# ScalarE's casts behind its copies, and row numbers counted from a partition's first row, in a DLRM tower kernel

## What is computed

```python
e = jnp.stack([tbl_0[ids[:, 0]], ..., tbl_26[ids[:, 26]]], axis=1)   # 2048 x 27 x 128
dot = jnp.einsum('bnd,bmd->bnm', e, e)                              # the pairs i < j are kept: 351
h = jnp.concatenate([pairs, dense_ctx], axis=1)                     # 2048 x 367
h = jnp.maximum(h @ W_top1 + b_top1, 0.0)                           # 512
h = jnp.maximum(h @ W_top2 + b_top2, 0.0)                           # 256
y = h @ W_top3
```

## Time and profile before

| | before |
|---|---|
| median of 3 runs | 383.83 us (383.69 to 386.02) |
| the profiled execution: its time, its span | 381.17 us, 379.3 us |
| PE busy in the span | 345.7 us (91%) |
| PE busy in 0 to 89 us, and in 89 to 363 us | 63.38 us of 89; 271.19 us of 274 |
| VectorE, ScalarE, POOL busy | 294.4, 153.3, 269.3 us |
| ScalarE busy in 0 to 89 us | 37.95 us |
| mean granted clock of PE | 0.987 |

### The profile page before, as it was taken

How to read it: one execution, slowest core, us unless ns; L and a number is a source line. 1 busy time by engine, 2 the same in 40 slices (tenths; PEclk the granted TensorE clock), 3 DMA queues, 4 the chain that set the end, 5 groups by cost and what they waited for, 6 DMA issues and landing times.

```text
span 379.3 us, 9954 instructions
## 1 busy us (share of the span) xinstructions
PE 345.7 (91%) x4035; PEld 322.6 (85%) x4035; DVE 294.4 (78%) x821; ACT 153.3 (40%) x217; POOL 269.3 (71%) x287
## 2 busy tenths in 40 slices
PE   1788868599999999999999999999999999999985
PEld 1677767588999999998999999998999999998874
DVE  4986696898688969798689969798689869793432
ACT  3352644434343453534343453534243453533421
POOL 6777877777777777777777777777777777777400
PEclk9989996999999999999999999999999999999999
DMA  6995225953333333334333333333343343221100
GB/s 184 251 247 136 64 63 137 213 186 96 82 93 85 79 84 82 95 69 95 82 94 85 79 86 81 95 72 91 85 91 85 76 89 83 76 57 50 36 2 1
DMA packets 22988, 36.38 MB, mean 96 GB/s; under 512 B 6224, under 2 KB 17120, under 8 KB 22944
## 3 DMA queue, kind: packets, MB, share of 16 engines
q0 software_dynamic: 8896, 18.24, 20.2%
q1 hardware_dynamic: 14048, 17.52, 18.6%
HBM read 35.73 MB, written 0.01 MB: 94 GB/s over the span
## 4 chain that ended last, share of the span: by engine, by line
PE 75%; POOL 14%; issue 5%; DMA 3%; ACT 2%; DVE 1%; ACTq 0%; DVEq 0%
PE embT_ps L410 35%; PE gram_ps L442 13%; POOL emb L379 12%; PE h_ps L470 11%; PE h_ps L494 7%; PE embT_ps L420 6%; DMA emb<-in_tbl,idx 3%; PE flat_ps L453 2%; POOL flatT L379 2%; ACT embT L634 1%; DVE flat L568 1%; DMA idx<-in_idx_rows 0%; PE h_ps L481 0%; PE flat_ps L481 0%; DVE flat L569 0%
## 5 line engine op out<-in xcount | busy, mean ns | idle before, releaser
L379 POOL DMA_INDIRECT emb<-in_tbl,idx x272 | 261.8, 962 | 83.8 <-issue 80.6
L537 DVE TENSOR_SCALAR one_hot<-ids,row_of 125x256 fp32r<-125x256 int32 x658 | 205.4, 383 | 13.2 <-PE embT_ps L410 10.6
L410 PE MATMUL embT_ps<-one_hot,tbl 125*128 125x256 f32 x1284 | 182.0, 297 | 13.0 <-DVE one_hot L537 11.4
L410 PEld LDWEIGHTS embT_ps<-one_hot,tbl 125*128 125x128 f32 x1284 | 166.7, 196 | 17.9 <-issue 8.9
L634 ACT COPY embT<-embT_ps 128x256 f32<-128x256 f32 x77 | 48.0, 624 | 134.2 <-PE embT_ps L410 129.0
L642 ACT COPY embT<-embT_ps 128x512 f32<-128x512 f32 (+1 forms) x80 | 80.7, 1012 | 11.7 <-PE embT_ps L420 11.7
L568 DVE STREAM_TRANSPOSE flat<-gram_ps 128x864 f32<-128x864 f32 x31 | 33.5, 1082 | 43.7 <-PE gram_ps L442 43.1
L442 PEld LDWEIGHTS gram_ps<-embT 128*59 128x59 f32 x1984 | 56.2, 134 | 9.6 <-ACT embT L634 3.9
L442 PE MATMUL gram_ps<-embT 128*59 128x54 f32 x1984 | 60.2, 217 | 3.8 <-ACT embT L634 2.3
L420 PE MATMUL embT_ps<-ident,emb 128*128 128x128 f32 x272 | 43.8, 276 | 11.6 <-DMA emb<-in_tbl,idx 8.6
L420 PEld LDWEIGHTS embT_ps<-ident,emb 128*128 128x128 f32 x272 | 32.2, 142 | 13.8 <-DMA emb<-in_tbl,idx 11.4
(11 more groups left out here) (47 smaller groups left out, 85.0 us busy)
## 6 DMA issues: line engine op xcount, KB each, us to landing
ids<-in_ids_hot SPq DMA_DIRECT2D x77, 128.0 KB
emb<-in_tbl,idx POOLq DMA_INDIRECT x272, 3.1
embT<-in_tbl SPq DMA_DIRECT2D x5, 448.0 KB
w_sb<-in_tbl SPq DMA_DIRECT2D x3, 560.0 KB
w_sb<-in_W_ring SPq DMA_DIRECT2D x1, 756.0 KB
w_sb<-in_W_top SPq DMA_DIRECT2D x1, 512.0 KB
h1T<-in_tbl SPq DMA_DIRECT2D x1, 448.0 KB
w_sb<-in_tbl SPq DMA_DIRECT2D x1, 448.0 KB
```

The source lines that it names most:

```text
L379: pool.indirect_dma_start(gathered_row(t, s), None, tables[f][:, :], bass.IndirectOffsetOnAxis(ap=idx[:, t, f:f + 1], axis=0),).then_inc(g ...
L410: mm = pe.matmul(out[:, 0:HN], tbl[0:ROWS, part, AT[o] + chunk, :], one_hot[0:ROWS, k % SLOTS, c, :], start=(chunk == 0 and part == 0), st ...
L537: done = dve.tensor_scalar(one_hot[0:ROWS, k % SLOTS, c, :], of, row_of[0:ROWS, KINDS.index(CH[o]), chunk:chunk + 1], None, ALU.is_equal)
```

## The change

Two things are done, both in the first two halves of the samples.

- ScalarE's table casts move. Before, the cast of table n + 3 stood ahead of the copy of hot step n. Now that of table n + 2 stands behind the copy of hot step n; and the casts of tables 5 to 9 stand right behind the copy of hot step 6, 7, 8, 10 and 12, where they stood ahead of the copy of hot step 7, 8, 9, 11 and 13, with the copies of the quads in between.
- For the hot steps 0 to 16, ScalarE rewrites the ids in place: it makes the partition's first row minus the id, as a float (`relative_ids`). VectorE then compares with a constant, minus the number of the chunk, where it compared integer ids with a number per partition that it read from `row_of`. These are 17 new instructions on ScalarE; 56 + 86 = 142 compares of VectorE change their form (7 steps of 8 chunks; 7 of 8 and 3 of 10), and 516 do not.

```diff
+    RELATIVE = len(HOT0) + len(hots_of(1))
...
             def build(n):
                 _, _, o = HOTS[n]
                 of = ids[0:ROWS, n % IDS, :]
-                dve.wait_ge(ids_loaded[n % IDS], 16 * (n // IDS + 1))
+                if n < RELATIVE:
+                    dve.wait_ge(ids_relative, n + 1)
+                else:
+                    dve.wait_ge(ids_loaded[n % IDS], 16 * (n // IDS + 1))
...
-                        done = dve.tensor_scalar(one_hot[0:ROWS, k % SLOTS, c, :], of,
-                                                 row_of[0:ROWS, KINDS.index(CH[o]), chunk:chunk + 1], None,
-                                                 ALU.is_equal)
+                        columns = one_hot[0:ROWS, k % SLOTS, c, :]
+                        if n < RELATIVE:
+                            done = dve.tensor_scalar(columns, of.bitcast(F32), float(-chunk), None, ALU.is_equal)
+                        else:
+                            done = dve.tensor_scalar(columns, of, row_of[0:ROWS, KINDS.index(CH[o]), chunk:chunk + 1],
+                                                     None, ALU.is_equal)
...
+            def relative_ids(n):
+
+                act.wait_ge(ids_loaded[n % IDS], 16 * (n // IDS + 1))
+                if n == 0:
+                    act.wait_ge(rows_ready, len(KINDS))
+                kind = KINDS.index(CH[HOTS[n][2]])
+                act.activation(ids[0:ROWS, n % IDS, :].bitcast(F32), ids[0:ROWS, n % IDS, :], ACT.Identity,
+                               bias=row_of[0:ROWS, kind, 0:1], scale=-1.0).then_inc(ids_relative, 1)
...
             AHEAD = 3
+            LEAD = 2
             for o in range(AHEAD):
                 split_high(o)
+                relative_ids(o)
             for kind, *of in ORDER:
                 if kind == "hot":
                     n = READ["hot", of[0], of[1]]
-                    if n + AHEAD < WHOLE:
-                        split_high(n + AHEAD)
-                    elif n in SPLIT_AT:
-                        split_high(SPLIT_AT[n])
                 if kind == "quad":
                     copy_quad(*of)
                 elif kind == "hot":
                     copy_hot(*of)
+
+                    if AHEAD <= n + LEAD < WHOLE:
+                        split_high(n + LEAD)
+                    elif n + 1 in SPLIT_AT:
+                        split_high(SPLIT_AT[n + 1])
+                    if AHEAD <= n + LEAD < RELATIVE:
+                        relative_ids(n + LEAD)
```

More of the change, by code:

```diff
@@ L281, in dlrm_tower @@
         low_ready = sem("low_ready")
+        ids_relative = sem("ids_relative")
         ids_loaded = [sem(f"ids_loaded{b}") for b in range(IDS)]
```

## The result

The change makes the kernel slower by a little: 384.78 us (median of 22 runs, 382.19 to 388.98) against 381.98 us for the kernel before (22 runs, 380.35 to 386.02). The ratio is 1.0069 with a 95% interval of 1.0045 to 1.0092. With 22 runs the kernel before came out 1.85 us lower than the median of three that the forecast started from, so the difference, +2.80 us, is larger than the forecast +1.9, while the time itself is 0.9 us under the forecast 385.7.

A forecast was written before the change was run, and what follows sets the result against it. POOL's gathers bound the kernel to about 81 us, PE's own work after, with 1.1 us of slack. Terms 0 + 0 + 0 + 1.9 took the profiled 381.17 to 383.1, the median 383.83 to 385.7 us; range 382.0 to 388.4.

The forecast's parts named there:

- the forecast +1.9: Whole kernel: net loss from POOL's lateness beyond PE's slack, +2.0 us, taken as +1.9 for slightly earlier loads; chance 0.44.
- The last gather was to be issued some 3 us later: Sign that the forecast is right: POOL's last gather issued some 3 us later relative to the first than before.
- PE's last long wait for a gather was to end at 83 to 84 us: Sign that the forecast is right: PE's last long gather wait ends there, with the same work behind it.
- the slack: PE at the third quad of even tiles: 1.1 us (0.7 to 1.5) by which POOL may be late without cost.
- the tight quads: Third quad of the even tiles: in tile 6 the last gather is issued 3.89 us before PE turns it.
- the step from 3.1 to +2.0: At the tight quads: POOL 3.1 us late, less PE's 1.1 us to spare, costs +2.0 us.
- Shorter compares: VectorE's 142 compares: 0.05 us less each, 7 us in all; gain on the path 0, up to 2 without cover.
- Seventeen instructions on ScalarE: ScalarE: 0.45 us each, 8 us; dots of 39.32 come 1.5 us later, delay gone by 61 us; cost 0 to 1.5.
- the sign that was to speak for ScalarE's queue: Sign of a wrong forecast: PE idle at 39 to 43 us and late from there without POOL being late.
- Copies ahead of casts: PE's wait of 1.29 us at 18.03 goes, the gather wait at 30.16 grows instead; gain 0.
- Where the subtractions fall: Subtractions 2 to 5, near 10 to 21 us, leave POOL's step and hold gathers: 3.1 us lost, +1.9 taken.
- Rival 1: Gathers beside dense compares also held: 25 x 0.09 = 2.3 us on top, +4.2, 388.0 us; chance 0.19.

The follow-up runs named there:

- experiment 3: First five subtractions replaced by copies of zeros out of PSUM: in the changed kernel 382.37 us (ratio 1.0006), in the kernel before 382.01 us (0.9985).
- all six executions: Profiled executions of the kernel before, the changed kernel, experiment 3 in both, experiment 4, and the kernel before with one load moved; times 381.17 to 384.08 us.
- experiment 4: Changed kernel whose compares in the first 17 hot steps read a number per partition again: median 383.46 us, ratio 1.0007 to the kernel before.
- experiments 3 to 5: experiment 3, experiment 4, and the kernel before with the second layer's weights loaded six ids later: 382.14 us against 381.94, ratio 1.0021.
- the kernel after with memsets: Changed kernel with all ten subtractions replaced by memsets of the low parts, on a chip with long transfers: 580.26 us, ratio 0.9959.
- the order alone (second group): Kernel before with only the casts moved behind the copies, compares unchanged, on a second chip with long transfers: 565.77 us against 562.61, no ratio.

## Why the prediction was right, point by point

- **The forecast as a whole.** The direction held, the time lies inside the range, and the part of the change that was named as its cause, the place of the subtractions, is the one whose removal takes the cost away (experiment 3). The way from there to the time did not come as worked out. Two of the signs that were named failed. The last gather was to be issued some 3 us later relative to the first, and it came 0.90 later (352.81 us behind it instead of 351.91); PE's last long wait for a gather was to end at 83 to 84 us, and it ended at 73.14. That +1.9 came near the measured +2.8 is in part luck.
- **What bounds the kernel, and the slack.** Behind 89 us PE is its own bound, as I had said, and it goes through that stretch in 281.60 to 281.72 us in all six executions. That POOL's lateness beyond 1.1 us costs PE time at the tight quads, the step from 3.1 to +2.0, is borne out by no trace: POOL was never late enough relative to PE, and PE waits for no gather between 91 and 360 us. I had also read the quad at 81.35 as the end of a long wait for POOL; PE waited 0.41 us there, and 2.88 at 75.83.
- **Shorter compares.** Forecast 0.05 us each, 7 us in all; by the medians (0.281 against the 0.342 of the earlier trace rows) it is 0.06, the upper bound, and VectorE's busy time fell by 11.5 us, more than 142 x 0.06 = 8.5. I had not counted that a compare is held up less itself. At the wait I had looked at it is worth nothing, as forecast: PE still waits 1.86 us for VectorE at 56.04, and then 2.56 for the gather at 60.74. But a gain of 0 was too little. In the hot steps of ten chunks, where PE hardly waits, it took 6.81 us from 81.77 to the pair products at 88.58, and now 5.88 from 83.42 to 89.30: 0.9 us that hides a part of the loss. With long compares again, in experiment 4, the chain of waits has such a step at 3.13 us, as before; with short ones, in experiment 3, at 2.41.
- **Seventeen instructions on ScalarE.** Forecast 0.45 us, measured 0.503. The pair products behind hot step 6 began at 41.81 instead of 39.32, 2.5 us later, where I had said 1.5; PE's wait for ScalarE there grew by 1.3 (2.03 against 0.71), the rest is lateness from before it. This is near the sign that was to speak for ScalarE's queue (PE idle at 39 to 43 us). But POOL was late too, by 1.10 us at its 31st gather, and PE's delay was given up at the waits of 48.54 and 60.26, as forecast, but for half a microsecond: its quads there begin at 49.16 and 60.74. That the same queue costs nothing in experiment 3 confirms it.
- **Copies ahead of casts.** No gain, as forecast: the wait at 18.03 went, and waits of 3.71 and 2.67 us for gathers came at 20.91 and 27.42. PE did feel POOL and the transfers in the first 30 us, where I had said that it would not: the quad of 30.16 begins at 31.34.
- **Where the subtractions fall.** That they would leave POOL's rhythm and hold its gathers was right, and their starts were walked to within 0.3 us. The sizes: 0.97, 0.30, 0.55 and 0 us, 1.8 in sum, for 0.9, 0.4, 0.85 and 0.95, 3.1 in sum. The fifth was luck of 0.01 us. I had also counted the first as unchanged; its hold of 1.03 us went in this execution, because the gather came 0.15 us earlier. POOL's net lateness is 1.10 us at the 31st gather and 0.74 at the last, not 3.1. This term was the one that was mis-sized.
- **What the sum left out.** Rival 1's smaller hold is real: 17 gathers in 0 to 89 us, each begun about 0.07 us behind a compare, take some 0.08 longer, 1.4 us, where the rival had 25 x 0.09 = 2.3. Each goes on 0.12 to 0.13 us before the compare's end, which leaves 0.08 of a compare of 0.28 that began 0.07 earlier. The long compares of the earlier trace rows do this in 3 gathers only; one that begins 0.07 us ahead of a gather takes 0.39 us itself and holds none. The rival's loss belongs beside the subtractions, not against them. With the zeros from PSUM there are 19 such gathers and 1.6 us, and the time still returns, so these holds alone don't cost.
- **The size in all.** The change costs 2.80 us where +1.9 was forecast. The profiled execution shows 0.72 us of PE's lateness at 89 us and 1.7 of a lower clock in the last 11 us, and it lies 1.3 us under the median of its runs. What the typical execution loses beyond it is in no trace and stays open. The granted clock doesn't carry it all: nine executions of the changed kernel at 0.978 average 385.0 us, and eight of the kernel before at 0.978, from the groups of experiments 3 to 5, average 382.0.

## What to carry to other kernels

A faster instruction can cost time through where it puts its neighbours. Where one engine paces a part of the kernel with a fixed beat (here a gather each 1.25 us), look in the timeline at what starts just ahead of that beat on the engine it contends with: a subtraction 0.01 us ahead of a gather, time after time, is a rhythm, and an edit of 0.06 us can break it. To test for it, keep the instruction's length and change what it touches (operand from PSUM) instead of taking it out. And don't take a shift that two engines share for one holding the other: ask the waits of the later stage, and a second execution of the same program, before you call it the path.

## What the runs showed of the hardware

- A memset into SBUF on VectorE, 0.91 us, held a gather's issue for 0.90 us; one of the others, at 17.75 in the kernel after with memsets, held none. A copy of 1.23 us from PSUM into SBUF, begun 0.08 to 0.95 us ahead of five gathers, held none. The Trainium skill ("SBUF — State Buffer", Who interferes with whom) says that an instruction of VectorE with at most one SBUF input outside the two-port modes doesn't contend with GpSimd; by it the memset should have been free, and the measurement decides against it, while the PSUM copy agrees.
- A subtraction with both inputs in SBUF holds a gather that starts 0.07 us or more behind it, by up to 1.03 us for 1024 columns; the gather goes on 0.12 to 0.13 us before the subtraction's end. A gather recorded 0.01 us behind a subtraction's start was never held, and the subtraction took 0.04 us longer instead (1.27 and 1.23). At 0.04 us both occur: the gather of 42.89 in the kernel before is held and takes 2.00, the one of 6.56 in the order alone (second group) takes 0.95. The same section of the Trainium skill says that the order of issue decides who blocks. The pairs with the gather first agree; the pairs 0.01 us apart, with the subtraction first by its recorded start, don't, unless recorded starts are no measure of the order at that distance.
- A compare of 256 columns of 0.28 us holds a gather begun 0.07 us behind its start by 0.08 us: this gather, too, goes on 0.12 to 0.13 us before the compare's end (17 gathers in 0 to 89 us of the kernel after).
- On VectorE a constant in place of a number per partition takes 0.06 us off a compare of 125 x 256. It is the operand and not the type: with float ids and a number per partition, in experiment 4, the median is again 0.343 us, as this row by line shows.

```profile
L545 DVE TENSOR_SCALAR one_hot<-ids,row_of x142: 332/343/552, 7.8 to 87.8; 125x256 fp32r<-125x256 f32 x142
```
